# Placing a mixture-of-experts' tokens inside the slots of a gather instead of after it, on one core

## What is computed

```python
x = x + gnn0(layernorm(x), src, dst, edge_weight)          # 100000 edges
x = x + ffn0(layernorm(x))                                 # top-k tokens, gelu
x = x + gnn1(layernorm(x), src, dst, edge_type_16)         # gated messages of 16 relations, relu
xf = layernorm(x)
gate_logits = xf @ Wg + bg                                 # 6250 x 8
top_w, top_i = top_k(gate_logits, 2);  top_w = softmax(top_w)
w_dense = sum(one_hot(top_i, 8) * top_w[..., None], axis=1)
for e in range(8):                                         # W1[e]: 256 x 1024, W2[e]: 1024 x 256
    out = out + w_dense[:, e:e + 1] * (gelu(xf @ W1[e] + b1[e]) @ W2[e] + b2[e])
x = x + out
```

## Time and profile before

| | us |
|---|---|
| median of 3 runs | 3400.14 |
| lowest, highest | 3399.47, 3401.7 |
| span of the profiled execution | 3402.6 |

### The profile page before, as it was taken

How to read it: one execution, slowest core, us unless ns; L and a number is a source line. 1 busy time by engine, 2 the same in 40 slices (tenths; PEclk the granted TensorE clock), 3 DMA queues, 4 the chain that set the end, 5 groups by cost and what they waited for, 6 DMA issues and landing times. The chain is left out here.

```text
span 3402.6 us, 59974 instructions
## 1 busy us (share of the span) xinstructions
PE 2615.4 (77%) x14271; PEld 1921.6 (56%) x14272; DVE 1733.1 (51%) x5663; ACT 723.6 (21%) x1907; POOL 1869.7 (55%) x1915
## 2 busy tenths in 40 slices
PE   7688888887777799999655555564555389999997
PEld 6577777776665344444344444443444267767774
DVE  6455545454554655555355454544544544545553
ACT  4121111111110233333211010000000233333332
POOL 1777777777774000000377777777777245555554
PEclk9899999998999899999888888777777689999998
DMA  7333333333332444444545454555544623222232
GB/s 224 110 113 113 113 111 111 113 113 113 110 113 67 173 197 192 188 191 194 194 141 155 151 154 142 152 154 151 146 146 146 241 59 48 45 45 48 45 48 33
DMA packets 175589, 434.08 MB, mean 128 GB/s; under 512 B 41712, under 2 KB 103792, under 8 KB 169232
## 3 DMA queue, kind: packets, MB, share of 16 engines
q0 software_dynamic: 97072, 236.21, 26.9%
q1 hardware_dynamic: 57424, 183.78, 14.1%
q10 hardware_dynamic: 21008, 13.24, 1.3%
HBM read 275.05 MB, written 158.04 MB: 127 GB/s over the span
## 5 line engine op out<-in xcount | busy, mean ns | idle before, releaser
L776 POOL DMA_INDIRECT g_msg<-table,idx x1564 | 1517.3, 970 | 518.8 <-issue 476.5
L848 PE MATMUL psum<-g_msg,g_hot 128*128 x3328 | 967.4, 456 | 593.0 <-SPq L719 358.1
L848 PEld LDWEIGHTS psum<-g_msg,g_hot 128*128 128x128 f32 x3328 | 756.5, 233 | 789.5 <-issue 654.5
L796 DVE TENSOR_SCALAR g_hot<-iota,g_cols 128x128 f32<-128x128 f32 x1664 | 450.1, 364 | 31.9 <-DVE g_cols L793 30.5
L1908 POOL DMA_INDIRECT out<-ex_y,ex_to x112 | 206.0, 1839 | 253.9 <-DMA out<-ex_y,ex_to 165.3
L768 POOL MEMSET g_origin<- 128x256 f32 x1 | 0.3, 313 | 590.8 <-POOLq L1359 590.8
L1594 PE MATMUL psum<-wrel_halves,t_xhi 128*128 128x512 f16 x784 | 298.2, 380 | 1.7 <-DVE t_row L1475 1.7
L1595 PE MATMUL psum<-wrel_halves,t_xhi 128*128 128x512 f16 x784 | 298.1, 380 | 0.0
L1596 PE MATMUL psum<-wrel_halves,t_xlo 128*128 128x512 f16 x784 | 298.1, 380 | 0.0
L1475 DVE TENSOR_SCALAR t_row<-psum,t_gate 128x256 f32<-128x256 f32 x392 | 171.2, 479 | 233.7 <-PE psum L1596 231.7
L2074 PE MATMUL psum<-w,ex_ghi 128*128 x784 | 260.6, 382 | 6.7 <-DVE ex_y L1983 6.4
(11 more groups left out here) (353 smaller groups left out, 3231.7 us busy)
## 6 DMA issues: line engine op xcount, KB each, us to landing
table<-t_row SPq DMA_DIRECT2D x48, 2048.0 KB, 6.3
g_msg<-table,idx POOLq DMA_INDIRECT x1564
piece_stage<-in_w SPq DMA_DIRECT2D x32, 512.0 KB, 5.7
w_halves<-piece_halves SPq DMA_DIRECT2D x32, 512.0 KB, 3.4
w<-w_halves SPq DMA_DIRECT2D x8, 2048.0 KB, 22.6
rows<-sc_row ACTq DMA_DIRECT2D x50, 128.0 KB, 2.2
out<-acc ACTq DMA_DIRECT2D x49, 128.0 KB
table<-t_row SPq DMA_DIRECT2D x24, 256.0 KB, 2.5
```

What stands on the lines that cost most here:

```text
L776: pool.indirect_dma_start(out=msg[:, at:at + D], out_offset=None, in_=table, in_offset=bass.IndirectOffsetOnAxis(ap=t[f"idx{g}"][:, n:n + ...
L796: last = nc.vector.tensor_scalar(hot[b][:, k * P:(k + 1) * P], t["iota32"][:, :], c3[:, k, where:where + 1], c3[:, k, weight:weight + 1], ...
L848: pe.matmul(ps, hot[b % PAIR][:, k * P:(k + 1) * P], msg[:, bass.ds(slot_at[k], D)], start=False, stop=False, skip_group_check=True).then_ ...
```

## The change

**Picks and places move into the slots.** `Score` gets three VectorE steps per slot, in the order `ranks`, `picks`, `low`, `counted`, and then add and norm as before. `picks` finds the two best experts of the 128 tokens of the last window with 13 linked operations of 128x8 or less. `counted` waits for TensorE's count (two f16 matmuls of 8 columns: tokens before each one in the window, and all of the window) and adds them to a running base per expert. `ranks`, a slot later, turns the counts into a row and a column for each pick and writes six blocks: `row_no` and `row_share` (128x128, twice) and `col_hot` (128x404, twice). TensorE's `place` sums with four f32 matmuls of 404 columns the token numbers (bank 6) and the differences of the two logits (bank 7) into PSUM, where they stay up to the end. An expert has 50 columns (`SPAN`) there, whatever its count, and two columns for empty places are at the end. TensorE's slot now does transposes and logits in the same slot. ScalarE copies the transposed rows first and forms the row's high part after the row before has landed.

**After the gather** VectorE ends the last slot, works out from the final counts the `owner` and the first column (`place`) of each tile, and reads banks 6 and 7 in a few operations of 128x404: `node_at`, `node_to`, and, in one pass, the share of each place, 1 / (1 + exp of the difference), with ScalarE's Abs and Exp. The facts and their transfer are gone, and so is `shares` in `experts`. A row has 256 words.

**In the experts' loop** the column of a tile is no longer 2n: `place(eng, n)` loads it into a register, on GpSimd before either copy and on VectorE once for each tile. The first four fetches take the same way with copies of their indices.

**The weights' load is in two parts.** `begin` asks for the 23 of 32 pieces whose memory lies in `acc` and `side` of the first 48 windows, and for the biases, as soon as the last piece has been stored and 48 windows' x is stored. `end` asks for the other 9 after the last row and the last x are stored.

The core of the diff:

```diff
 class Score:
+    def ranks(self, dve, n, tile):
...
+        dve.wait_ge(self.placed, n)
+        for k in range(TOP):
+            link(nc.vector.tensor_tensor_reduce(out=self.spare[:, :], in0=self.hot[k][:, :], in1=self.rank[:, :], scale=1.0, scalar=0.0,
+                                                op0=ALU.mult, op1=ALU.add, accum_out=self.ids[:, k:k + 1]))
+        link(nc.vector.tensor_scalar(self.ids_i[:, :], self.ids[:, :], col(const["off"], tile), None, ALU.add))
...
+        for k in range(TOP):
+            at, to = self.part[:, TOP + k:TOP + k + 1], self.part[:, k:k + 1]
+            nc.vector.tensor_scalar(self.row_no[k][:, :], self.t["iota32"][:, :], at, col(const["number"], tile), ALU.is_equal, ALU.mult)
+            nc.vector.tensor_scalar(self.row_share[k][:, :], self.t["iota32"][:, :], at, self.diff[:, k:k + 1], ALU.is_equal, ALU.mult)
+            last = nc.vector.tensor_scalar(self.col_hot[k][:, :], const["col_no"], to, None, ALU.is_equal)
+        last.then_inc(self.hots_done, 1)
+    def counted(self, dve, n):
...
+        dve.wait_ge(self.ranked, n)
+        nc.vector.tensor_tensor(self.rank[:, :], self.psD, self.base[:, :], ALU.add).then_inc(self.ranked_link, 1)
...
     def vector(self, dve, n, begun, ended, last, before_last):
-        self.logit(dve, n, before_last)
+        self.ranks(dve, n, before_last)
+        self.picks(dve, n, last)
         self.low(dve, n)
+        self.counted(dve, n)
...
     def tensor(self, pe, n):
-        self.score(pe, n)
+        self.count(pe, n)
+        self.place(pe, n)
         pe.wait_ge(self.norm.done, n)
...
+    def place(self, pe, n):
+        pe.wait_ge(self.hots_done, n)
+        for k in range(TOP):
+            for ps, rows in ((self.psN, self.row_no), (self.psS, self.row_share)):
+                last = pe.matmul(ps, rows[k][:, :], self.col_hot[k][:, :], start=False, stop=False, skip_group_check=True)
+        last.then_inc(self.placed, 1)
...
 class Place:
     def sync(self, sp):
-        sp.dma_start(self.table[:, :], self.dram["place_table"]).then_inc(self.consts_in, 16)
-        sp.wait_ge(self.score.out_done, WINDOWS + self.score.LAST)
-        sp.wait_ge(self.score.stored, 16 * (WINDOWS + 1))
         sp.wait_ge(self.core.x_stored, 16 * WINDOWS)
-        self.load(sp)
+        self.load[0](sp)
+        sp.wait_ge(self.score.paired, WINDOWS + 1)
+        sp.wait_ge(self.score.stored, 16 * (WINDOWS + 1))
+        sp.wait_ge(self.core.x_stored, 16 * (WINDOWS + 1))
+        self.load[1](sp)
...
 def experts(core, t, dram, free, w1, w2, b1, b2, out):
+    def place(eng, n):
+        at = t["place"][0:1, n:n + 1] if isinstance(n, int) else t["place"][0:1, bass.ds(n, 1)]
+        return eng.value_load(at, min_val=0, max_val=Score.EMPTY)
...
-            def fetch(n, b):
-                core.hold(pool, "pool", turned, n + 1)
-                core.hold(pool, "pool", share_done, n + 1)
+            def fetch(n, b, first=False):
+                c = place(pool, n)
+                if not first:
+                    core.hold(pool, "pool", turned, n + 1)
...
             def add(n, b):
+                c = place(pool, n)
...
-                dve.wait_ge(share_done, n + 1 + AHEAD)
                 dve.wait_ge(y_free, n + 1)
...
-                    nc.vector.tensor_scalar(y[b % 2][:, s * D:(s + 1) * D], whole[s][:, :], share[b][:, s:s + 1], None, ALU.mult).then_inc(y_done, 1)
+                    nc.vector.tensor_scalar(y[b % 2][:, s * D:(s + 1) * D], whole[s][:, :], share[s], None, ALU.mult).then_inc(y_done, 1)
...
-def load_experts(core, sp, dram, w1, w2, b1, b2):
+def load_experts(core, dram, w1, w2, b1, b2, places):
+    gone = [(places["acc"], places["acc"] + 4 * (WINDOWS - 1) * D), (places["side"], places["side"] + 4 * (WINDOWS - 1) * D)]
+    inside = lambda at: any(a <= at and at + bytes_of <= b for a, b in gone)
+    early = [[n for n in range(own) if inside(base + n * bytes_of)] for base in (first, second)]
+    rest = [[n for n in range(own) if n not in some] for some in early]
```

More of the change, by code:

```diff
@@ L820, in _ @@
                 then.vector(dve)
-            else:
-                for k in range(1, follow.LAST):
-                    follow.vector_last(dve, k)
         @block.tensor
@@ L1668, in __init__ @@
-        self.equal, self.rest, self.run = (keep.sb(f"pl_{k}", [P, self.COLS], F32) for k in ("equal", "rest", "run"))
-        self.hot = [keep.sb(f"pl_hot{k}", [P, self.COLS], F16) for k in range(TOP)]
-        self.best, self.which = ([keep.sb(f"pl_{k}{i}", [P, WINDOWS], F32) for i in range(TOP)] for k in ("best", "which"))
-        self.one = keep.sb("pl_one", [P, WINDOWS], F32)
-        self.full, self.ends, self.start = (keep.sb(f"pl_{k}", [P, EXPERTS], F32) for k in ("full", "ends", "start"))
@@ L1809, in tensor @@
[L1809 to L1828 removed]
+        chain(nc.vector.tensor_scalar(self.jump[:, :], self.full[:, :], -1.0 / P, float(score.SPAN), ALU.mult, ALU.add))
```

459 lines of the change are left out of this document (207 added, 252 removed).

## The result

The changed kernel is slower: 3505.61 us (median of 4 runs, 3505.02 to 3508.18) against 3400.92 for the kernel before in the same runs, a ratio of 1.0312 (95% interval 1.0297 to 1.0327). The profiled execution has a span of 3503.5 us, 100.9 more than before.

The account below looks back on a forecast made before the run. GpSimd was taken to bound the gather (1.281 us a tile), with next to no slack against TensorE in the experts. 3402.6 - 22.4 + 3 + 5 = 3388.2, less 2.5 for the runs' median: 3386 us, range 3364 to 3414.

Parts of the forecast that it names:

- Part 1: Hand-over to the experts: weights requested earlier, so the first up matmul comes at 2717 instead of 2739.4, gain 22.4 us.
- Part 2: Hand-over: the placement is hidden under the weights' transfer; TensorE could start at 2706.5, some 10 us before the weights let it.
- the 1.1 us for one: Hand-over: upper price of one f32 place matmul of 404 columns, making the four 1.5 to 4.3 us.
- Part 3: Gather: the longer slots fit into a turn and cost +3 us, between 0 and +15.
- +15: Gather: upper end of the slots' cost, 0.3 us a turn, for GpSimd's descriptors held up beside VectorE's new operations.
- Both fit, barely: Gather turn of 19.3 us: VectorE's work is 18.2 us and TensorE's 15.8 to 19.2.
- The ring: Gather: of 32 messages (41 us), about two batches, some 18 us, are slack before GpSimd stops.
- Part 4: Experts' loop: an exposed register load of 0.4 us on GpSimd costs +5 us, between -10 and +32.
- the 31 us: Experts' loop: upper cost of the exposed load by the skill's 600 ns floor, 0.6 x 52.
- D: Rival: slots bound the gather, VectorE and TensorE waiting for each other; turns of 19.8 give 3409, 20.1 give 3425; chance 0.14.
- C: Rival: GpSimd's register loads set the experts' pace, slower or no gain; 3413 at a loop of 12.0 us; chance 0.18.
- B: Rival: the register loads hide and the experts' loop settles at TensorE's pace, 3371 us; chance 0.16.

Follow-up runs that it names:

- e6: Changed kernel with the split of the weights' pieces one batch later and TensorE's count taken a slot later: 3397.06 us, 0.9988 of the kernel before.
- e9: e6 with own semaphores for 16 of 19 linked operations of a slot, VectorE's loop 309 instead of 357 instructions: 3388.41 us, 0.9962 of the kernel before.
- e14: The kernel of e9 run again: 3389.05 us, 0.9954 of the kernel before.
- e15: e9 with weights' pieces of the first 40 windows' memory requested before the gather's end, behind the last piece's load: 3389.67 us, 0.9956 of the kernel before.
- e20: e9 with 60 empty semaphore instructions, executed once, between VectorE's two loops, so the second lies elsewhere: 3392.99 us, 0.9970 of the kernel before.
- e4: Changed kernel with one matmul of 8 columns instead of the four place matmuls in each slot (only the gather is comparable): 3542.92 us, gather 1150 us.
- e5: Changed kernel with VectorE taking TensorE's count at the head of the next slot: 3438.74 us, 1.0107 of the kernel before.
- e2: Changed kernel with each piece of weights split one batch later: 3428.79 us, 1.0082 of the kernel before.
- e16: Kernel before with the pieces' split one batch later and the changed kernel's bounded register loads: 3403.88 us, 1.0002 of the kernel before.
- e7: Kernel before with 53 empty semaphore instructions behind each slot's norm on VectorE, loop 357 instead of 198 instructions: 3421.27 us, 1.0056 of the kernel before.
- e17: e9 with GpSimd's register load of the place between second fetch and copy made twice: 3390.38 us, 0.9965 of the kernel before.

## Why the prediction was wrong

**Part 1, the weights: right.** Forecast was a first up matmul 22.4 us earlier against the gather's end; it is 23.7. The transfer took from 2790.08 to about 2839.8, 49.7 us instead of 45.9, and began 7.2 us before the last product where the sum had 3.2 (2670.15 - 2667): that the two nearly cancel is luck.

**Part 2, the placement: just hidden, with none of the cover that I gave it.** From the last norm (end about 2803.3) to the first up matmul are 39.5 us, where I had 31.1 without the weights (2706.5 - 2675.4); TensorE's first turn waits for the fetch, which lands 0.5 us after the weights. The forecast of the hand-over came out all the same, since the two ends fell together; that is luck too. The chain of VectorE and TensorE was to end 17.9 us after the last norm (2693.3 - 2675.4) and ends 27.7 after it, at 2830.97. Ten of these us are two waits of VectorE for which the sum had nothing:

```profile
2809.03 0.17 DVE L1167 CUSTOM_DVE_ANT_0 pl_spare<-pl_hot,pl_rank 128x8 f32<-128x8 f32 x1 [5.71 <-issue]
...
2820.11 0.17 DVE L1167 CUSTOM_DVE_ANT_0 pl_spare<-pl_hot,pl_rank 128x8 f32<-128x8 f32 x1 [4.31 <-PE psum L1285]
```

The first, which the profile can't name, stands behind the last slot in e6, e9 and e14 too (5.4 us), and not in e15 and e20; what it is wasn't tried. The second is for the place matmuls, of which four take 5.8 us here, at a lower clock, and 3.0 in most slots; the 1.1 us for one, that is 4.3 for four, on which the sum put its upper end stood in no row.

**Part 3, the slots: here the prediction failed.** The term was +3 with an upper bound of +15, and it is +127. The prices weren't off: ranks, picks and low part are 7.2 us as priced, the place matmuls lie beside the norm (e4), and a slot is 12.4 us of VectorE where I had 12.1. Nor was it GpSimd's descriptors held up beside VectorE: L775 takes 976 ns where it took 977, so the +15 end has no part in the 127 us. The step that failed is "Both fit, barely". It set a sum of work, 18.2 us, against a mean turn, 19.3, and took the difference for slack, as if VectorE could do its work at any time within a turn. It can't.

(1) It waits in the slot for TensorE's count, which comes after two batches of products, and the hot blocks of the next two batches stand behind that wait: e5 shows 67 us for taking that wait away. I named this wait and then left it without a price.

(2) The pieces of weights. Rows 3 showed VectorE 15.00 us idle before L647, released by the load of the piece, and the view of waits of before has 185.2 us of it in 16 times:

```profile
DVE piece_halves L647 <- DMA piece_stage<-in_w: 185.2, 16, 16.9
```

I read that as idle time and so as room for the slot. It is a wait for SyncE, which waits for TensorE's products, and work that is put behind it can't be moved into it: e2 shows 77 us, e16 that it cost nothing before. Together they are 108.5 us (e6).

(3) The turn back of a loop of 357 instructions costs VectorE 3.3 us, 14 times, for which no row of before could have warned, since a loop of 198 doesn't have it (e7).

Of what is left after (1) and (2), 20 us of the gather, e9 takes 12 away, the stalls of GpSimd. The other 8 are the cost for which the +15 stood: once GpSimd sets the pace again, its 782 fetches take 8 us longer than before in e9 and 13 in e20, about as much as the time from its first message to its last grows (1009.6 and 1014.3 us, 1001.8 before). So a part of the bound was sound, and the lost turns hid it in the changed kernel.

The ring was the other mistake: 18 us of slack were taken as cover for each turn, but slack of a ring is used once. A turn that is 2 us too long has eaten it after nine turns; GpSimd's first stall ends at 1809, some seven turns after its start.

**Part 4, the experts' loop: sign and mechanism wrong, small.** +5 was forecast for an exposed register load, and the stage is 2.5 us shorter. The copy begins where the second fetch ends, with the load between them, as it did without one:

```profile
2902.27 0.98 POOL L1871 DMA_INDIRECT ex_xin<-rows,ex_idx  x1 [0.30 <-issue]
2903.26 0.19 POOL L1877 COPY ex_to<-node_to 128x2 int32 x1
2904.47 1.62 POOL L1886 DMA_INDIRECT out<-ex_y,ex_to  x1 [1.03 <-issue]
```
```profile
3439.58 2.22 POOL L1886 DMA_INDIRECT out<-ex_y,ex_to  x1 [1.02 <-issue]
```

(2902.27 + 0.98 = 2903.25, and the copy starts at 2903.26.) The mean over 47 tiles is (3439.58 - 2904.47) / 47 = 11.39, the same as before; why the stage is 2.5 us shorter, no run shows. A gap of 0 behind an indirect DMA doesn't say that the next instruction's preparation took no time; it is hidden behind the 0.98 us, and e17 hides two. The Trainium skill, DMA: Bandwidth & Descriptors, section "Latency and other measured facts", has about 600 ns as the floor of a `tensor_load`; nothing here contradicts that duration, but the 31 us that I worked out by it were wrong, because none of it is exposed.

**The rivals.** D was the right one: the slots bound the gather, and VectorE and TensorE wait for each other. It had 0.14, and I priced it for turns of 19.8 and 20.1; they became 21.3 in the first part and 23.8 in the second. The price of a us was right (the mean turn is 22.2 us where it was 19.3, which in 47 turns is 134 us, and the gather is 129 longer), the size wasn't, and the range ended where D began to count. Of C nothing was seen, and B's mechanism (the loads hide) held, but its gain didn't come: the loop kept its 11.39.

## What to carry to other kernels

Work may be put into an engine's idle time only after asking what that idle time waits for: time behind a wait for a load, whose request itself waits for the engines that are served, is no room (185.2 us here). A sum of work below a turn's length says nothing where the same turn holds a wait on another engine in its middle; take results of another engine a turn later, where they are long there (e5), and place a step that needs a load as late as its consumer allows (e2). And when a loop's body grows, look at the "issue" gap at its turn back and at the packets of the instruction queue.

## What the runs showed of the hardware

A long body of a loop is fetched again each time it turns back: 198 instructions on VectorE cost nothing (15 packets on the instruction queue), 357 cost 2.9 to 3.9 us each time in the changed kernel (90 packets), and 309 did or didn't depending on where they lay (54 packets in e9, 19 in e20). The Trainium skill, Runtime: NRT & Kernel Launch, section "Instruction fetch mechanics", says that a taken branch whose target is outside the two blocks that an engine holds forces a fetch before it can go on; the traces agree with that, the place of the loop included.

An empty semaphore increment on VectorE costs 5.20 / 53 = 0.098 us. A register load on GpSimd behind an indirect DMA costs nothing (e9, e14), nor do two (e17).

What VectorE does lengthens GpSimd's indirect DMAs. Of the 782 of the gather, none that had VectorE idle beside it took over 0.96 us in before, the changed kernel, e9, e14 and e20, and each one that took over 1.4 us (9, 10, 13, 17 and 23 of them; the longest 1.66) ran beside VectorE's split of a piece, where the mean is 1.15 to 1.29 us. The Trainium skill, SBUF — State Buffer, section "SBUF: two separate sides", has the two engines share one port pair as an exclusive lock; the traces agree with it as far as the split goes, though no run tested it by itself. It had no part in the 127 us.

Less work on TensorE went with a lower clock: in e4 it was busy 592.6 us of 1149 in the gather at a mean granted clock of 0.70, in the changed kernel 700.2 of 1129 at 0.77 (1.0 is 2.4 GHz, and 0.5 the lower of its two levels).
